# Perceiver layer on one core: latent attention on each sequence's own 64 keys, and Wr streamed in the position product

## What is computed

```python
# second layer: I = 16 positions, B = 64, H = 8 heads of F = 128
pe = _sinusoid_pe(I, D, x.dtype)[::-1]
r = (pe @ Wr).reshape(I, H, F)
pos = jnp.einsum('ibnf,jnf->ijbn', q + v_bias, r)
# third layer, latent attention: S = 64, NH = 16 heads, HH = 16, HD = 32
kv_lat = xn @ W_kvd
q_lat = xn @ W_qd
...
v = (kv_lat @ W_vu).reshape(B, S, NH, HD)
...
scores = jnp.einsum('bqhd,bkhd->bhqk', qq, kk) * scale
scores = jnp.where(causal[None, None], scores, jnp.finfo(scores.dtype).min)
probs = jax.nn.softmax(scores, axis=-1)
y = jnp.einsum('bhqk,bkhd->bqhd', probs, v).reshape(B, S, H)
return y @ W_o
```

## Time and profile before

| | us |
|---|---|
| three runs | 930.94, 932.64, 936.75 |
| median | 932.64 |
| the profiled execution | 932.9 |
| its span | 931.0 |
| TensorE busy with products in the span | 847.3 (91%) |
| VectorE busy | 512.5 (55%) |
| GpSimd busy | 341.8 (37%) |
| ScalarE busy | 308.4 (33%) |

### The profile page before, as it was taken

One profiled execution on the slowest core, in us unless ns is written; L12 is line 12 of the kernel. 1 busy time (PEld: TensorE's weight loads), 2 busy tenths in 40 slices (PEclk: granted clock), 3 DMA queues, 4 the chain that ended last, 5 costly groups with the idle time before them and its releaser, 6 DMA issues.

```text
span 931.0 us, 15960 instructions
## 1 busy us (share of the span) xinstructions
PE 847.3 (91%) x6048; PEld 624.6 (67%) x6049; DVE 512.5 (55%) x1113; ACT 308.4 (33%) x820; POOL 341.8 (37%) x172
## 2 busy tenths in 40 slices
PE   1799999999899998979989999799999999997982
PEld 1555554555497688968757667478878888886871
DVE  7666787666531254534776776874554343432425
ACT  2222333232422155641065666642321112121211
POOL 0000000001525424540015234443349999993051
PEclk8899999999879999999989999999999999998995
DMA  9847765556020030020195000003157434550254
GB/s 352 322 182 284 283 242 223 218 210 236 20 89 1 25 114 1 1 75 1 66 397 215 1 0 0 1 21 117 46 216 258 161 136 144 191 201 25 68 157 159
DMA packets 46698, 127.03 MB, mean 136 GB/s; under 512 B 4000, under 2 KB 8096, under 8 KB 40752
## 3 DMA queue, kind: packets, MB, share of 16 engines
q1 hardware_dynamic: 37744, 106.29, 30.8%
q10 hardware_dynamic: 6336, 11.54, 3.5%
q0 software_dynamic: 2560, 8.39, 2.7%
HBM read 102.05 MB, written 24.15 MB: 136 GB/s over the span
## 4 chain that ended last, share of the span: by engine, by line
PE 73%; DVE 8%; POOL 8%; DMA 5%; issue 3%; ACT 2%; another core or an unknown queue 1%; SPq 0%; POOLq 0%; DVEq 0%; ACTq 0%
PE scores L479 10%; PE bank L506 8%; PE bank L963 4%; PE bank L965 4%; PE bank L964 4%; DMA nat<-in_ctx_keys 3%; POOL ring_lo L1178 3%; PE bank L779 2%; POOL ring_hi L1176 2%; PE bank L736 2%; PE bank L792 2%; PE bank L554 2%; PE bank L634 2%; PE bank L702 2%; DVE ctxT L1564 2%
## 5 line engine op out<-in xcount | busy, mean ns | idle before, releaser
L1564 DVE STREAM_TRANSPOSE ctxT<-nat 128x1024 f32<-128x1024 f32 (+3 forms) x120 | 120.7, 1067 | 5.6 <-DMA nat<-in_ctx_keys 5.5
L479 PE MATMUL scores<-ctxT,hn 32*64 32x385 f32 (+2 forms) x2048 | 94.9, 512 | 13.3 <-DVE ctxT L1564 13.2
L506 PE MATMUL bank<-nat,probT 128*64 128x512 f32 (+1 forms) x416 | 94.1, 598 | 0.0
L1057 POOL TENSOR_TENSOR wq_lo<-wq_raw,wq_hi 128x1024 fp32r<-128x1024 f32 x4 | 9.3, 2351 | 227.3 <-ACT wq_hi L1251 227.3
L479 PEld LDWEIGHTS scores<-ctxT,hn 32*64 32x64 f32 x2048 | 65.8, 134 | 38.6 <-issue 27.5
L1104 POOL TENSOR_TENSOR sp<-sp,s_inv 128x512 f32<-128x512 f32 x32 | 32.6, 1039 | 140.9 <-DVE s_inv L1869 140.9
L1178 POOL TENSOR_TENSOR ring_lo<-ring_raw,ring_hi 128x2048 fp32r<-128x2048 f32 x18 | 82.9, 4604 | 1.4
L963 PE MATMUL bank<-ring_hi,xg_lo 128*128 x176 | 73.3, 416 | 0.4 <-DVE y L2085 0.4
L965 PE MATMUL bank<-ring_hi,xg_hi 128*128 x176 | 69.5, 395 | 0.0
L964 PE MATMUL bank<-ring_lo,xg_hi 128*128 x176 | 69.1, 392 | 0.0
L1176 POOL TENSOR_TENSOR ring_hi<-ring_raw,cst 128x2048 fp32r<-128x2048 f32 x18 | 64.9, 3604 | 8.7 <-DMA ring_raw<-in_Wexp 8.7
(11 more groups left out here) (280 smaller groups left out, 1991.5 us busy)
## 6 DMA issues: line engine op xcount, KB each, us to landing
nat<-in_ctx_keys SPq DMA_DIRECT2D x46, 1024.0 KB, 7.3
ring_raw<-in_Wexp SPq DMA_DIRECT2D x21, 1024.0 KB, 9.5
x_slots<-zeros SPq DMA_DIRECT2D x1, 5632.0 KB, 27.1
y_slots<-zeros SPq DMA_DIRECT2D x1, 5632.0 KB, 38.5
hn<-x_slots ACTq DMA_DIRECT2D x22, 256.0 KB, 3.1
y_slots<-hn ACTq DMA_DIRECT2D x22, 256.0 KB, 2.1
w_raw<-in_Wexp SPq DMA_DIRECT2D x3, 1024.0 KB, 11.0
nat<-in_ctx_keys SPq DMA_DIRECT2D x16, 130.0 KB
```

What stands on the lines that cost most here:

```text
L479: last = nc.tensor.matmul(scores4[64 * b:64 * b + 64, i, 0:KEYS_IN[i]], q4[rows_i, j, 64 * b:64 * b + 64], ctxT[rows_i, b, j, 0:KEYS_IN[i] ...
L506: last = nc.tensor.matmul(bank[7][64 * b:64 * b + 64, :], probT[0:n, j, 64 * b:64 * b + 64], nat[k % 2][0:n, b, j, :], start=j == 0, stop= ...
L1564: dve.transpose(dst, src).then_inc(columns_ready, 1)
```

## The change

**Position product.** The roles are swapped: the position table, padded to 32 columns (16 of them zero), is the weights, and Wr is streamed, 256 columns at a time, two heads to each of the four 32-column strips (L582 to L586 of the kernel after). The result has the positions as rows (`r_rows`), so behind keys(0, 4) two transposes turn it, and VectorE copies it to rT_pad in the order of heads; the memset of rT_pad is gone, since the padding is zero already.

**Scores.** Each sequence is scored against its own 64 keys: for each quad two products, one per sequence b, with that sequence's 64 query columns as weights and 256 streamed columns (four heads of 64 keys), into its half of the array's columns and of PSUM's partitions. So eight heads fill a bank, `halves` f = 0, 1 take the place of quads, each half has a bank of its own, and the mask is laid once a half. Maxima, reciprocals and GpSimd's products are done eight heads at a time, exps have 64 columns. kT_h's columns are placed so that sequence b's keys come together (KEY_PLACES).

**Weights and values.** sp_ holds [two heads x 64 keys], so one transpose turns two heads: eight in place of sixteen, one copy to spT on each engine. The values go to `v_own`, cleared once, block-diagonal: heads 2i and 2i + 1 of sequence b, rows 0 to 63 for the one and 64 to 127 for the other. For that the value projection is four products of 64 x 256, W_vu comes with even heads first, and ScalarE copies in two pieces. self_output is sixteen products of 64 columns of weights by 64 streamed columns.

**Semaphores and places.** Counts go from four a step to two; GpSimd clears v_own too; `zeros` moves by 1 KB.

The diff, cut to its core:

```diff
+KEY_PLACES = [slice(0, 6, 5), slice(1, 5, 3), slice(2, 8, 5), slice(3, 7, 3)]
...
-    c[:, C_CAUSAL:C_CAUSAL + P] = np.where((p // 64 == q // 64) & (q <= p), 0.0, NEG)
+    c[:, C_CAUSAL:C_CAUSAL + SQ] = np.where(q[:, 0:SQ] <= p % SQ, 0.0, NEG)
...
+        def own_values(t, half):
+
+            at = slice(0, 34 * HD) if half == 0 else slice(HD, 31 * HD)
+            blocks = t[SQ * half:SQ * (half + 1), at].rearrange("p (b r d) -> p b r d", b=2, d=HD)
+            return blocks[:, :, 0:2 * PAIRS - 1:2, :]
...
-                    for m in range(NH):
-                        for c in range(HC):
-                            last = nc.tensor.matmul(bank[2][:, m * SEQ:(m + 1) * SEQ], wr_sb[:, c, m * F:(m + 1) * F],
-                                                    cst[:, C_PE + c * SEQ:C_PE + (c + 1) * SEQ], start=c == 0, stop=c == HC - 1)
+                    for c in range(HC):
+                        for q in range(4):
+                            last = nc.tensor.matmul(bank[2][B32 * q:B32 * (q + 1), 0:2 * F],
+                                                    cst[:, C_PE + c * B32:C_PE + (c + 1) * B32],
+                                                    wr_sb[:, c, q * 2 * F:(q + 1) * 2 * F], start=c == 0, stop=c == HC - 1,
+                                                    skip_group_check=True)
+                    last.then_inc(rT_full, 1)
...
+                if n == 5:
+                    pe.wait_ge(rT_ready, 1)
+                    for h in range(2):
+                        last = nc.tensor.transpose(bank[2][:, (2 + h) * F:(3 + h) * F], r_rows[:, h * F:(h + 1) * F], ident)
...
-                nc.tensor.matmul(bank[3][:], latT[par][:, 0, :], wvu_sb[:], start=True, stop=True).then_inc(vv_full, 1)
+                for b in range(2):
+                    for f in range(2):
+                        odd = D // 2 * (b ^ f)
+                        last = nc.tensor.matmul(bank[3][SQ * f:SQ * (f + 1), D // 2 * b:D // 2 * (b + 1)],
+                                                latT[par][:, 0, SQ * b:SQ * (b + 1)], wvu_sb[:, odd:odd + D // 2],
+                                                start=True, stop=True, skip_group_check=True)
+                last.then_inc(vv_full, 1)
...
-            def self_scores(t, par, quads):
+            def self_scores(t, par, halves):
                 pe.wait_ge(kTh_ready, t + 1)
-                for c in quads:
-                    b = score_bank(t, c)
+                for f in halves:
                     if not (isinstance(t, int) and t == 0):
-                        pe.wait_ge(sexp_ready, 4 * t + c - 1)
-
-                    nc.tensor.matmul(b[:], ident_bf[:], causal_bf[:].rearrange("p n q -> p (n q)"), start=True,
-                                     stop=False)
-
-                    nc.tensor.matmul(b[:], qT_h[par][:, c, :], kT_h[par][:, c, :, :].rearrange("p n q -> p (n q)"),
-                                     start=False, stop=True).then_inc(self_full, 1)
-
-            def weight_columns(k, par, quads):
-                for c in quads:
-                    pe.wait_ge(sp_ready, 4 * k + c + 1)
-                    if c >= 2:
-                        pe.wait_ge(spT_dve if c % 2 else spT_act, 2 * k + 1)
-                    elif c == 0 and not (isinstance(k, int) and k == 0):
-                        pe.wait_ge(xx_ready, k)
-                    elif isinstance(k, int) and k == 0:
-                        pe.wait_ge(sexp_ready, c + 3)
-                    for n in range(4):
-                        last = nc.tensor.transpose(bank[6 + c % 2][:, n * P:(n + 1) * P], sp_[par][:, 4 * c + n, :], ident)
-                    last.then_inc(spT_full, 1)
+                        pe.wait_ge(sexp_ready, 2 * t + f - 1)
+
+                    nc.tensor.matmul(bank[4 + f][:], ident_bf[:], causal_bf[:].rearrange("p n q -> p (n q)"), start=True,
+                                     stop=True)
+                    for i in range(2):
+                        for b in range(2):
+                            own = slice(SQ * b, SQ * (b + 1))
+                            last = nc.tensor.matmul(bank[4 + f][own, i * D // 2:(i + 1) * D // 2], qT_h[par][:, 2 * f + i, own],
+                                                    kT_h[par][:, 2 * f + i, 4 * b:4 * b + 4, :].rearrange("p n q -> p (n q)"),
+                                                    start=False, stop=True, skip_group_check=True)
+                    last.then_inc(self_full, 1)
+
+            def weight_columns(k, par, f):
+                pe.wait_ge(sp_ready, 2 * k + f + 1)
+                if f == 0 and not (isinstance(k, int) and k == 0):
+                    pe.wait_ge(xx_ready, k)
+                for i in range(4):
+                    last = nc.tensor.transpose(bank[6 + f][:, i * P:(i + 1) * P],
+                                               sp_[par][:, 8 * f + 2 * i:8 * f + 2 * i + 2, :].rearrange("p n q -> p (n q)"), ident)
+                last.then_inc(spT_full, 1)
...
-                pe.wait_ge(spT_act, 2 * k + 2)
-                pe.wait_ge(spT_dve, 2 * k + 2)
-                for h in range(HEADS):
-                    last = nc.tensor.matmul(bank[0][HD * (h % 4):HD * (h % 4 + 1), h // 4 * P:(h // 4 + 1) * P],
-                                            v_t[par][:, HD * h:HD * (h + 1)], spT[:, h, :], start=True, stop=True,
-                                            skip_group_check=True)
+                pe.wait_ge(spT_act, k + 1)
+                pe.wait_ge(spT_dve, k + 1)
+                for b in range(2):
+                    for i in range(PAIRS):
+                        at = b * D + i * 2 * HD
+                        last = nc.tensor.matmul(bank[0][SQ * (i % 2):SQ * (i % 2 + 1), i // 2 * P + SQ * b:i // 2 * P + SQ * (b + 1)],
+                                                v_own[par][:, at:at + 2 * HD], spT[:, i, SQ * b:SQ * (b + 1)], start=True, stop=True,
+                                                skip_group_check=True)
...
-                weight_columns(k, par, (0, 1))
+                weight_columns(k, par, 0)
                 if project:
                     latents(k + 2, par)
                 if scores:
                     key_columns(k + 1, 1 - par)
-                weight_columns(k, par, (2, 3))
+                weight_columns(k, par, 1)
                 if project:
                     rotary_keys(par)
                 if scores:
-                    self_scores(k + 1, 1 - par, (0, 1))
+                    self_scores(k + 1, 1 - par, (0,))
                 self_output(k, par)
                 if project:
                     from_latents(k + 2, par)
                 if scores:
-                    self_scores(k + 1, 1 - par, (2, 3))
+                    self_scores(k + 1, 1 - par, (1,))
...
+                for f in range(2):
+                    pool.wait_ge(sinv_ready, 2 * k + f + 1)
+                    at = slice(8 * f, 8 * f + 8)
+                    nc.gpsimd.tensor_tensor(sp_[par][:, at, :], sp_[par][:, at, :],
+                                            s_inv[par][:, at].unsqueeze(2).broadcast_to([P, 8, SQ]), ALU.mult).then_inc(sp_ready, 1)
...
-                nc.scalar.copy(v_t[par][:], bank[3][:]).then_inc(vv_ready, 1)
+                for half in range(2):
+                    last = nc.scalar.copy(own_values(v_own[par], half),
+                                          bank[3][SQ * half:SQ * (half + 1), :].rearrange("p (b r d) -> p b r d", b=2, d=HD))
+                last.then_inc(vv_ready, 1)
...
+            def self_exps(k, par, halves):
+                for f in halves:
+                    act.wait_ge(sbias_ready, 2 * k + f + 1)
+                    for n in range(8):
+                        h = 8 * f + n
+                        last = nc.scalar.activation(sp_[par][:, h, :], bank[4 + f][:, n * SQ:(n + 1) * SQ], ACT.Exp,
                                                     bias=s_bias[par][:, h:h + 1], scale=SELF_SCALE,
                                                     accum_out=s_sum[par][:, h:h + 1])
...
-            chain(dve.memset(rT_pad[:], 0.0))
-            dve.tensor_copy(rT_pad[:, :, 0:SEQ], bank[2][:, 0:NH * SEQ].rearrange("p (n j) -> p n j", n=NH)).then_inc(rT_ready, 1)
+            dve.tensor_copy(r_rows[:], bank[2][:, 0:2 * F]).then_inc(rT_ready, 1)
+            dve.wait_ge(rT_full, 2)
+            dve.tensor_copy(rT_pad[:].rearrange("p (q h) j -> p q h j", h=2),
+                            bank[2][:, 2 * F:4 * F].rearrange("p (h q j) -> p q h j", h=2, j=B32)).then_inc(rT_ready, 1)
...
+            def self_max(k, par, halves):
+                for f in halves:
+                    dve.wait_ge(self_full, 2 * k + f + 1)
+                    at = slice(8 * f, 8 * f + 8)
+                    chain(dve.tensor_reduce(s_max[par][:, at], bank[4 + f][:].rearrange("p (n q) -> p n q", n=8), AX,
```

104 lines of the change are left out of this document (44 added, 60 removed).

## The result

| | before | changed kernel |
|---|---|---|
| median of four runs, us | 933.56 | 909.57 (905.77 to 912.72) |
| ratio, 95% interval | | 0.973 (0.969 to 0.977) |
| the profiled execution, its span | 932.9, 931.0 | 910.3, 908.5 |
| TensorE busy | 847.3 (91%) | 814.3 (90%) |

The change saves 24.0 us. The forecast was 904 with a range of 894 to 915: the time lies inside, 5.6 above the forecast. To see where the span's 22.5 us came from I cut both traces at the same five points of TensorE's program, each read from the timeline: the start of norm_transposes(7), of norm_columns(0), of weight_columns(1), of weight_columns(6), and of the first shared expert product.

A forecast was written before the change was run, and what follows sets the result against it. TensorE, 73% of the last-ending chain, was taken as the bound, with the ScalarE and VectorE loop also tight in latent attention. Position product 11.4, entry 3.9, five steps 8.1 and exit 5.0 sum to 28.4: 932.9 to 904, range 894 to 915.

The forecast's parts named there:

- The step: Latent attention, one 128-token tile: a loop through four engines, forecast to go from 17.8 to 16.2, 1.6 a step.
- E: In the latent attention step: the end of the second-half scores, from which the loop's times are counted; exps forecast at E + 1.1.
- changes of width: Strip-width switches on TensorE in latent attention: six a step instead of two, four more at 0.07, 0.3 a step.
- Five steps: Latent attention from the end of step 0 to that of step 5: 1.6 a step, 8.1 saved.
- Entry: Start of latent attention and step 0: query columns 2.1 earlier, plus 1.8 in step 0's scores and transposes, 3.9 saved.
- rival 1: Latent attention: ScalarE or VectorE takes the step, second-half exps wait for heads_out; step 17.0, time 910; chance 0.17.
- Exit: End of latent attention: the 3.37 wait for exps goes, shared_hidden starts about 5 earlier, bounds 2 and 8.
- full drains: TensorE drains a record's full tail at each strip-width change: six cost 1.0 a step, not 0.4; time 4 us more.
- 2: Rival: waits at latent attention's entry and exit vanish and the clock stays; 35 saved, time 897; chance 0.10.
- 3: Rival: only the position product pays, the latent attention step stays at 17.8; time 921; chance 0.05.
- 4: Rival: strips and halves do not overlap in position product and latent attention; time 939, slower; chance 0.04.
- 5: Rival: TensorE's clock falls in the latent attention loop, costing 2.7 a step; time 923; chance 0.06, 0.02 of it slower.

The follow-up runs named there:

- e1: The kernel before with the new position product alone, latent attention as before: 927.62 against 937.72, ratio 0.989.
- e3: The kernel before, its old 16-column position products issued eight at a time ahead of each of keys(0, 4) to keys(0, 7): 932.16 against 937.72, ratio 0.995.
- e7: The changed kernel with each half's mask product made as two 64-column products side by side: ratio 0.974 to the kernel before, period 16.27.
- e8: The changed kernel with GpSimd's low part of the down weights made after the last step's work instead of during step 6: ratio 0.974 to the kernel before.
- e9: The changed kernel with useless mask products in TensorE's two long gaps, nine in step 0 and thirteen in step 6: 905.79, ratio 0.976 to the kernel before.
- e2: The changed kernel with the old position product, latent attention as changed: 923.61, ratio 0.985 to the kernel before.
- e4: The changed kernel with position products strip by strip and scores one 64-column half after the other: 916.91 against 937.72 for the kernel before, ratio 0.977.

## Why the prediction came out as it did

**Position product: right, for partly other reasons.** 11.4 forecast, 11.3 by e1 and the traces. The bound for strips that do not overlap is excluded by the 1.87 of L585. The division was off: the prediction put 2.4 on the clock, all of it behind the product; e3 shows 6.3, since most of the 16-column passes themselves ran at half clock. The total did not suffer, because the sum took out the whole 11.2 as measured.

**The step: mechanism right, 0.37 short.** The loop through four engines is the one that the trace shows: exps start at E + 1.05, the keys' copy ends the first-half wait, halves overlap. By terms: exps come every 0.29, not 0.28, which with the rest of that path puts the first mask product (0.32 ahead of L798) at E + 10.47 for 10.3 (+0.17). Mask and scores take 1.23 and 1.33 for 1.1 (+0.13, +0.23), the products from the latents 2.50 for 2.2 (+0.30), the values 1.04 for 1.2 (-0.16), and the separate 0.3 for changes of width is already in these (-0.3). The term that failed is that 0.3. Without any change of width mask and scores take the forecast's 1.1 (1.09 in e7), and the prediction priced four more changes at 0.07; e7 shows 0.13 for one, and changes make up most of the 0.66 in the three places above.

**Five steps: 7.05 for 8.1.** Five times 17.83 - 16.57 is only 6.3. The other 0.75 no term of the sum has: step 5 of the kernel before took 18.56 and not 17.83, with a bias of VectorE standing 0.92 (590.20) until GpSimd's multiply ended at 591.09, and the changed kernel has no such stall there (16.51). Without this windfall the row would miss by 1.8.

**Entry: 2.3 for 3.9.** It has two halves. The query columns came 1.5 earlier in the stretch and not 2.1 (23.11 against 24.62 behind norm_columns(0)): two reduces are gone, but the first one now waits for the four products of its eight heads and starts 0.38 later. From there to weight_columns(1) the kernel won 0.8 and not 1.8 (20.55 against 21.38). The sum counted step 0's saved scores and transposes in full and left out the loop's new waits, which are in step 0 too: its second-half exps began at E + 1.5 (488.88 - 487.41), right behind the copies of heads_out on ScalarE, and TensorE then stood 0.99 for xx. That is rival 1's mechanism, in one step only. GpSimd has a part in it: the first-half bias stood 0.75 for a subtraction, so everything behind it on ScalarE came up to 0.6 later (an estimate: 0.75 less the usual 0.17).

**Exit: 2.9 for 5.** The wait of 3.37 went as forecast, and expert_columns(0) came 15 us after E as forecast (585.56 - 570.57 = 14.99). What failed is the stretch behind it: from there to the first shared expert product the forecast had about 1 us less than before, and it took 16.58 for 15.78. The products behind the gap ran at half clock for longer, because the clock was at 0.50 from 584 to 591 (before from 607 to 610): the output product took 4.60 (587.18 to 591.78) for 2.83, the eight transposes ahead of it 1.62 for 1.15. The forecast put the clock's fall at the exit at nothing new. VectorE's stall of 3.9 was there before as well (in the trace of before L1545 takes 3.83 beside GpSimd's 4.51), and I read over it; e8 shows that it makes 2.0 of the gap of 3.19, and e9 that the gap costs 2.65 through the clock.

**The total.** The four stretches fall 4.7 short of the 28.4; the rest of the 5.6 is in the main the base, since the median of the kernel before was 933.56 in this comparison and not 932.64. The 908 that the prediction had for full drains is near the 909.57 by chance: it adds nothing at the entry and the exit, where 3.7 of the 4.7 are.

**Rivals.** 2 (waits vanish and the clock stays) did not happen at either end. 3 is out by e2, 4 by L585 and e4, and 5 in the loop: the clock is 1.00 in it, with idle gaps of 0.64. But the argument against 5, that the clock "fell before only after idle of 2.5 and 3.4 us", was wrong: at the position product it fell with TensorE busy, in rows that the prediction had read, and after the wait of 2.54 in the second layer it fell in ten profiles and stayed in four. The loop did keep its clock, but not for the reason given.
